# State loop of a selective scan: one half's product with B kept in PSUM and scanned there first, the skip term at the first state, and an order table for longer states

## What is computed

```python
xz = x @ W_in.T; u, z = split(xz, 2)
uc = silu(conv1d(u, conv_w, width 3) + conv_b)
proj = uc @ W_xproj.T; B, C, dt = proj[..., :16], proj[..., 16:32], proj[..., 32:]
delta = softplus(dt @ W_dt.T + b_dt); A = -exp(A_log)
h[t] = exp(delta[t] * A) * h[t-1] + (delta[t] * uc[t]) * B[t]
y[t] = sum over states of h[t] * C[t] + uc[t] * D
out = (y * silu(z)) @ W_out.T
```

## Time and profile before

| | |
|---|---|
| runs | 3148.79, 3151.88, 3153.04 us |
| profiled execution | 3154.66 us, span 3152.5 us |
| busy over the span | PE 2425.7 us (77%), DVE 2198.9 (70%), ACT 1710.0 (54%), POOL 1415.3 (45%) |
| first stage | 0 to 1249.76 us; DVE 118.5 of the 120 us from 400 to 520, 47.7 of the 70 from 520 to 590 |
| L344, scan | 128 instructions, 347.1 us, shortest 2257 ns, median 2280, longest 3610 |
| L379, addition on GpSimd | 120 instructions, 280.2 us, mean 2356 ns |
| L340, product with B | 128 instructions, 149.8 us, mean 1210 ns |

### The profile page before, as it was taken

One profiled execution on the slowest core, in us unless ns is written; L12 is line 12 of the kernel. 1 busy time (PEld: TensorE's weight loads), 2 busy tenths in 40 slices (PEclk: granted clock), 3 DMA queues, 4 the chain that ended last, 5 costly groups with the idle time before them and its releaser, 6 DMA issues.

```text
span 3152.5 us, 42236 instructions
## 1 busy us (share of the span) xinstructions
PE 2425.7 (77%) x15570; PEld 1750.1 (56%) x15570; DVE 2198.9 (70%) x3701; ACT 1710.0 (54%) x2608; POOL 1415.3 (45%) x1331
## 2 busy tenths in 40 slices
PE   3114776677667687799999999999999569876987
PEld 1002455344345565477777777777777456755675
DVE  3995698699699612588878887887888543355334
ACT  4223664666376242588777877787778323222332
POOL 0341144144224300365765676657656641564156
PEclk8556888788788888799999999999999879887988
DMA  3000000000000000100000010010000100000000
GB/s 100 0 0 0 0 1 1 1 1 1 1 1 1 1 1 14 41 21 21 21 21 21 21 28 21 20 26 21 21 24 9 41 1 1 1 14 1 1 1 14
DMA packets 32029, 42.02 MB, mean 13 GB/s; under 512 B 8897, under 2 KB 18130, under 8 KB 31442
## 3 DMA queue, kind: packets, MB, share of 16 engines
q1 hardware_dynamic: 31826, 39.34, 4.6%
HBM read 12.05 MB, written 2.10 MB: 4 GB/s over the span
## 4 chain that ended last, share of the span: by engine, by line
PE 46%; issue 19%; DVE 17%; POOL 12%; ACT 4%; SPq 1%; DMA 0%; POOLq 0%; ACTq 0%; DVEq 0%
PE ps L954 10%; PE ps L932 6%; PE ps L943 6%; POOL MA L379 5%; DVE MA L1090 3%; PE ps L710 3%; PE ps L914 2%; PE ps L1723 2%; DVE lnb L265 2%; PE ps L645 2%; PE ps L647 1%; PE ps L646 1%; PE ps L1665 1%; POOL MA L1173 1%; PE ps L1625 1%
## 5 line engine op out<-in xcount | busy, mean ns | idle before, releaser
L1090 DVE TENSOR_REDUCE MA<-ps 128x1 f32<-128x1024 f32 x512 | 623.3, 1221 | 195.3 <-PE ps L932 182.7
L379 POOL TENSOR_TENSOR MA<-MA,BIG 128x1024 f32<-128x1024 f32 x120 | 280.2, 2356 | 624.9 <-DVE BIG L350 624.9
L954 PE MATMUL ps<-MA,WB 128*64 128x128 f32 x4096 | 502.5, 276 | 0.0
L954 PEld LDWEIGHTS ps<-MA,WB 128*64 128x64 f32 x4096 | 440.7, 137 | 88.4 <-issue 87.4
L344 DVE TENSOR_TENSOR_SCAN BIG<-BIG 128x1024 f32<-128x1024 f32 x128 | 347.1, 2751 | 0.0
L932 PE MATMUL ps<-BIG 96*128 96x512 f16 x1024 | 314.6, 389 | 13.5 <-ACT WB L1017 5.1
L632 ACT ACTIVATE HR<-ps,b 128x512 f32<-128x512 f32 x288 | 191.6, 687 | 243.9 <-PE ps L647 242.9
L710 PEld LDWEIGHTS ps<-WB,HR 128*128 128x128 f32 x2304 | 307.3, 210 | 24.9 <-issue 8.6
L710 PE MATMUL ps<-WB,HR 128*128 128x128 f32 x2304 | 314.4, 295 | 0.0
L1017 ACT ACTIVATE WB<-ps,MA 128x1024 f32<-128x1024 f32 x206 | 229.6, 1115 | 149.8 <-DVE MA L1090 149.8
L497 PE MATMUL ps<-bc,sel 96*128 96x512 bf16 x256 | 108.3, 520 | 247.1 <-DVE BIG L350 190.8
(11 more groups left out here) (290 smaller groups left out, 5166.3 us busy)
## 6 DMA issues: line engine op xcount, KB each, us to landing
BIG<-BIG SPq DMA_DIRECT2D x192, 64.0 KB, 2.0
BIG<-WB SPq DMA_DIRECT2D x192, 64.0 KB, 2.0
WB<-w_dram SPq DMA_DIRECT2D x1, 2304.0 KB, 14.7
X<-x_dram SPq DMA_DIRECT2D x4, 512.0 KB, 12.6
HR<-w_dram SPq DMA_DIRECT2D x1, 2048.0 KB, 9.4
out_dram<-X SPq DMA_DIRECT2D x4, 512.0 KB, 3.2
WB<-wqkv_dram SPq DMA_DIRECT2D x1, 1536.0 KB, 6.7
WB<-w_dram SPq DMA_DIRECT2D x2, 512.0 KB, 9.1
```

Of the source, the lines that this page charges most:

```text
L379: e.tensor_tensor(yy[:, c, :], yy[:, c, :], db[n % 2][c], ALU.add).then_inc(*p_my.up(b, n, c))
L954: x = e.matmul(bank[6][64 * pp:64 * pp + 64, 0:128], V[(4 * b + g) % 2][:, k, 64 * pp:64 * pp + 64], DT[n % 2][:, 128 * k:128 * k + 128], ...
L1090: e.tensor_reduce(L_of(n)[:, c:c + 1], ps[s][:, :], AX, ALU.max, negate=True).then_inc(*v_amx.up(n, s))
```

## The change

1. The product of half 1 with B is written back to `ps[0]` in place; that of half 0 goes to SBUF as before. The scan of half 1 comes first and reads the PSUM tile. From then on half 1 precedes half 0 everywhere (scans, products with C, exponentials, additions, gate).
2. The matmuls of the next B row wait for the scan of half 1, no longer for the products with B.
3. The skip term is computed in state 0, behind the product with C; the gate waits for the last addition directly.
4. The tables are laid out for a state of 9.4 and an expert step of 9.4, and both batch periods are 222.

```diff
-        "wdt": 33.2, "exp": 39.2, "sp": 43.2, "du": 47.2, "n": 49.6, "dterm": 158.4, "gate": 162.4, "out": 164.4,
-        "rstats": 170, "rnorm": 173}
-M_PERIOD, N_PERIOD = 181, 6.8
-F_AT = {"stats": 0, "norm": 3, "tr": 9, "gate": 11, "top": 13, "wts": 16, "k": 18, "rstats": 18 + 8.8 * 18 + 9,
-        "rnorm": 18 + 8.8 * 18 + 12}
-F_PERIOD, K_PERIOD = 194, 8.8
+        "wdt": 33.2, "exp": 39.2, "sp": 43.2, "du": 47.2, "n": 49.6, "gate": 204, "out": 206.4,
+        "rstats": 210, "rnorm": 213}
+M_PERIOD, N_PERIOD = 222, 9.4
+F_AT = {"stats": 0, "norm": 3, "tr": 9, "gate": 11, "top": 13, "wts": 16, "k": 18, "rstats": 18 + 9.4 * 18 + 9,
+        "rnorm": 18 + 9.4 * 18 + 12}
+F_PERIOD, K_PERIOD = 222, 9.4
...
-                    e.tensor_tensor(db[k][c], du[:, c, :], ps[0][:, :], ALU.mult).then_inc(*v_mtb.up(b, n, c))
-                for c in range(2):
+                    e.tensor_tensor(db[k][0] if c == 0 else ps[0][:, :], du[:, c, :], ps[0][:, :], ALU.mult).then_inc(
+                        *v_mtb.up(b, n, c))
+                for c in (1, 0):
                     e.wait_ge(*a_mda.at(b, n, c))
                     e.wait_ge(*v_mtb.at(b, n, c))
-                    e.tensor_tensor_scan(db[k][c], da[k][c], db[k][c], 0.0, ALU.mult, ALU.add).then_inc(
-                        *v_mscan.up(b, n, c))
-                yield m_at(b, "n", N_PERIOD * n + 4.6)
+                    e.tensor_tensor_scan(db[k][c], da[k][c], db[k][0] if c == 0 else ps[0][:, :], 0.0, ALU.mult,
+                                         ALU.add).then_inc(*v_mscan.up(b, n, c))
+                yield m_at(b, "n", N_PERIOD * n + 7)
...
+                if n == 0:
+                    for c in (1, 0):
+                        e.wait_ge(*v_mth.at(b, 0, c))
+                        e.scalar_tensor_tensor(out=yy[:, c, :], in0=uc[:, c, :], scalar=small["dcol"][:, c:c + 1],
+                                               in1=yy[:, c, :], op0=ALU.mult, op1=ALU.add).then_inc(*dve_own.up())
+            yield m_at(b, "gate")
+            for c in (1, 0):
                 e.wait_ge(*p_my.at(b, 15, c))
-                e.scalar_tensor_tensor(out=yy[:, c, :], in0=uc[:, c, :], scalar=small["dcol"][:, c:c + 1],
-                                       in1=yy[:, c, :], op0=ALU.mult, op1=ALU.add).then_inc(*dve_own.up())
-                own[c] = dve_own.now()
...
-                yield m_at(b, "n", N_PERIOD * n + 4.6)
-                for c in range(2):
+                yield m_at(b, "n", N_PERIOD * n + 8.2)
+                for c in (1, 0):
...
-                        yield m_at(b, "n", N_PERIOD * (n - 1) + 2.3)
-                        e.wait_ge(*v_mtb.at(b, n - 1, 1))
+                        yield m_at(b, "n", N_PERIOD * (n - 1) + 4.7)
+                        e.wait_ge(*v_mscan.at(b, n - 1, 1))
```

More of the change, by code:

```diff
@@ L191, in program @@
         a_mva, a_mexp, a_mlog = tick("a_mva", NB, 2), tick("a_mexp", NB, 2), tick("a_mlog", NB, 2)
-        a_mda = tick("a_mda", NB, 16, 2)
+        a_mda = tick("a_mda", NB, 16, (1, 0))
         t_mtr, t_min, t_mwx, t_mwdt = tick("t_mtr", NB, 2), tick("t_min", NB, 8), tick("t_mwx", NB), tick("t_mwdt", NB, 2)
@@ L197, in program @@
         v_mx1, v_mbc, v_mu1, v_mdl = tick("v_mx1", NB), tick("v_mbc", NB), tick("v_mu1", NB, 2), tick("v_mdl", NB, 2)
-        v_mtb, v_mscan, v_mth = tick("v_mtb", NB, 16, 2), tick("v_mscan", NB, 16, 2), tick("v_mth", NB, 16, 2)
-        v_mgate = tick("v_mgate", NB, 2)
-        p_mrs, p_my, p_mx = tick("p_mrs", NB, ("in", "out")), tick("p_my", NB, range(1, 16), 2), tick("p_mx", NB)
+        v_mtb, v_mscan, v_mth = tick("v_mtb", NB, 16, 2), tick("v_mscan", NB, 16, (1, 0)), tick("v_mth", NB, 16, (1, 0))
+        v_mgate = tick("v_mgate", NB, (1, 0))
+        p_mrs, p_my, p_mx = tick("p_mrs", NB, ("in", "out")), tick("p_my", NB, range(1, 16), (1, 0)), tick("p_mx", NB)
         da = [[big[2 * k + c] for c in range(2)] for k in range(2)]
@@ L351, in mamba_dve @@
                         *v_mth.up(b, n, c))
-            yield m_at(b, "dterm")
-            for c in range(2):
-                e.wait_ge(*p_my.at(b, 15, c))
-                e.scalar_tensor_tensor(out=yy[:, c, :], in0=uc[:, c, :], scalar=small["dcol"][:, c:c + 1],
-                                       in1=yy[:, c, :], op0=ALU.mult, op1=ALU.add).then_inc(*dve_own.up())
-                own[c] = dve_own.now()
-            yield m_at(b, "gate")
-            for c in range(2):
-                e.wait_ge(*own[c])
+                if n == 0:
[5 more added lines that the diff above has]
+            for c in (1, 0):
+                e.wait_ge(*p_my.at(b, 15, c))
                 e.tensor_tensor(yy[:, c, :], yy[:, c, :], zs[:, c, :], ALU.mult).then_inc(*v_mgate.up(b, c))
@@ L401, in mamba_act @@
                     if k == 0 and b:
-                        e.wait_ge(*v_mgate.at(b - 1, 1))
+                        e.wait_ge(*v_mgate.at(b - 1, 0))
                     e.activation(zs[:, c - 2, 512 * h:512 * h + 512], bank[k % 4], ACT.Silu, bias=0.0,
@@ L415, in mamba_act @@
                 if c == 0 and b:
-                    e.wait_ge(*p_my.at(b - 1, 15, 1))
+                    e.wait_ge(*p_my.at(b - 1, 15, 0))
                 bd = small["bdt"][:, c:c + 1]
@@ L456, in mamba_pe @@
                     if b:
-                        e.wait_ge(*v_mth.at(b - 1, 15, 1))
+                        e.wait_ge(*v_mth.at(b - 1, 15, 0))
                 else:
@@ L490, in mamba_pe @@
                     elif k == 0:
-                        yield m_at(b, "n", N_PERIOD * (n - 1) + 2.3)
-                        e.wait_ge(*v_mtb.at(b, n - 1, 1))
+                        yield m_at(b, "n", N_PERIOD * (n - 1) + 4.7)
+                        e.wait_ge(*v_mscan.at(b, n - 1, 1))
                     else:
                         yield m_at(b, "n", N_PERIOD * n)
-                        e.wait_ge(*v_mth.at(b, n - 1, 1))
+                        e.wait_ge(*v_mth.at(b, n - 1, 0))
                     for h in range(2):
```

## The result

Eleven runs of each kernel gave medians of 3164.73 us for the changed one (3156.67 to 3172.59) and 3151.88 us for the one before (3148.37 to 3154.95): a ratio of 1.0041, 95% interval 1.0033 to 1.0050, so slower by 13 us. The forecast was 3169.9 us, between 3146 and 3184. The profiled execution took 3168.89 us, its span is 3166.6.

The account below looks back on a forecast made before the run. The vector engine bounds the loops, a chain through all engines the gaps. 84.94 + 152.6 + 3 x 180.5 + 3 x 107.7 + 165.6 = 1267.7 against 1249.76 us: +18, so 3169.9 us, range 3146 to 3184.

Parts of the forecast that it names:

- Batch 0's loop: From the loop's start to the gate's end in batch 0: 152.6 us, against 168.55 before.
- The contention with GpSimd: Scans held up by GpSimd's two additions lose 1.29 us a state; claimed gone in every state.
- so each state pays 0.12: Half 1's scan directly follows the product it depends on: starts 1.32 us apart instead of 1.20, making 9.01 us a state.
- I took nothing and kept 0 to 8 us: Extra cost of the product and scan using PSUM: counted as zero, with 0 to +8 us kept for the range.
- The tail of loops 1 to 3: From state 15's last scans to the gate's end in batches 1 to 3: 21.9 us each.
- the 6.8 us for the normalisations: In that tail, normalisations of 2.14 us were reckoned at 6.8 us beside two GpSimd additions.
- The gaps: Three stretches from a gate's end to the next loop: each 103.5 + d, or 107.7 us.
- I take the low clock to the end: In each gap TensorE stays at 1.2 GHz until the x-projections end, at 331.4 against 327.15 us: d = +4.2.
- d: Change in each gap's length against the first gap of before, 103.5 us; forecast +4.2 us.
- The bounds of -4.6 and +6: Limits of d per gap: -4.6 us if TensorE's clock never falls, +6 if low into the delta projection.
- Rivals 1 and 2: TensorE's clock holds in all gaps, 3143.5 us, chance 0.16; or in two of three, +0.4 us, chance 0.14.
- Rival 3: GpSimd holds off the PSUM scan like the SBUF one: 1.2 us in about 57 states, +68 us, chance 0.03.

Follow-up runs that it names:

- profile 1: First profiled execution of the changed kernel, nothing else edited: 3168.89 us, first stage 1264.1 us.
- profile 2: Second profiled execution of the same changed kernel, unedited: span 3155.8 us, first stage 1257.4 us; the ten runs of that repeat had median 3164.71 us.

## Why the prediction was right

- **Batch 0's loop.** 152.6 forecast, 153.7 measured. The contention with GpSimd went entirely, as said. The failed size is the dependent pair: "so each state pays 0.12". It pays 1.33 - 1.13 = 0.20. I had read the difference from the convolution's scalar-tensor instructions. There and here an independent instruction starts 0.08 to 0.09 us before the end of the one ahead of it, but the dependent one starts 50.56 - 50.52 = 0.04 us after that end in the convolution, all in SBUF, and 87.66 - 87.56 = 0.10 after it here, where the product goes through PSUM. Whether the further 0.06 is PSUM's or comes with the form of the pair no run separates. That is 16 x 0.08 = 1.3 us a batch; in loops 1 to 3 the tail, 0.9 us shorter than reckoned, takes most of it back. The sign against the Trainium skill's "VectorE: DVE Perf Modes", section "The DRAIN you can't avoid", held: it says of a row of copies that the semaphore after each costs nothing extra, and this trace shows 0.20 us where an instruction waits for the one just ahead of it, 12.8 us in 64 states.
- **PSUM.** I took nothing and kept 0 to 8 us; by the durations it is 2.0, from start to start of the two scans nothing. The TRN2 errata on the same page of the Trainium skill would give an estimate of 4 us for the 64 scans, 0.065 us each; the trace disagrees, they are 0.022 longer.
- **The tail of loops 1 to 3.** 21.9 us forecast, 21.0 measured, by the same chain. Most of the 0.9 is the 6.8 us for the normalisations: the row's own difference, 4.16 - 2.14 = 2.02 for one addition, gives 2.14 + 2 x 2.02 = 6.18 for two, and 6.18 is what they took. Moving the root and the normalisation alone gave 12 us a batch back.
- **The gaps.** The step "I take the low clock to the end" gave d = +4.2 and was too long in both profiles: no profile of this order shows a clock that stays low to the end of the projections. They stood between the quarters as 2, 2 and 4 matmuls, but the clock rose in the last group in profile 1 (106.1 - 103.5, d = +2.6) and amid the quarters in profile 2 (d = -0.6). The bounds of -4.6 and +6 held both. Rivals 1 and 2 asked whether the clock holds from one kernel to another; in fact the instant at which it rises differs between executions of one kernel.
- **The sum.** 1267.7 against 1264.1 us in profile 1, 3.6 less: the gaps 5.4 less, the other pieces 1.8 more. That all gaps follow the order of the first one is what made the kernel slower: two of them grew by 21.4 and 18.6 us, and the end got 24.9 shorter. Rival 3 (+68 us) fell with the first state's rows.
- **What I had left out.** The forecast took the length of the first gap as given. Its reason, that the mixture's head and first expert step stand ahead of the block's on three engines, was worth 25 to 28 us a gap, four times or more the largest bound that I weighed in d (+6).

## What to carry to other kernels

When an edit comes with a new table of the order, cost the two apart: here the operand in PSUM (with the skip term's move) gained 46 us and the order lost 60. In a gap that is one dependent chain, list what stands ahead of each of its instructions on every engine, and move what is not of the chain behind it; after that look for the next instruction that waits for someone else's result, since two of the three later places of the mixture made a new wait (7.05 and 8.04 us). Where a clock rises in a gap, read two profiles of the same kernel before a few us are given a cause.

## What the hardware showed that was not expected

- The same program with the same order has TensorE's clock rise 67.5 us after the gate's end in one execution and 75.6 us after it in another, 8 us apart, and each of the three gaps follows with about 3 us.
- A scan with two SBUF operands that starts while GpSimd adds two SBUF tensors waits until that addition ends: 56 of 56 ended 2.14 to 2.17 us after it, which makes the pairs of 5.76 us. A scan with one operand in PSUM takes 2.29 us beside the same additions, at most 22 ns more than one from SBUF without them. So the price goes by how much of GpSimd's instruction is left at the start, not by the length of one's own.
- Two gates that meet GpSimd's last addition take 4.48 us, 2.35 alone; in the kernel before it was the skip terms that met it, with 4.54 us as in the run with the skip term at its old place. The wait is not gone from the tail, it only changed its instruction.
